# Message stage of a two-layer graph network: roots by logarithm and exponential on ScalarE, and one more sum on VectorE

## The reference, cut to what matters

```python
def logmap(x, y):
    xy = jnp.clip(mink_dot(x, y) + K, None, -EPS) - K
    u = y + xy * x * C
    normu = jnp.clip(mink_norm(u), MIN_NORM, None)   # a square root
    dist = jnp.sqrt(sqdist(x, y))                    # arcosh: a square root and a logarithm
    return proj_tan(dist * u / normu, x)
...
x_local_tangent = logmap(x[row], x[col])
cat = jnp.concatenate([x_tangent[row], x_tangent[col], distances], axis=-1)
h = jax.nn.silu(cat @ att_w1 + att_b1)
att = jax.nn.sigmoid(h @ att_w2 + att_b2) * edge_mask
agg = jax.ops.segment_sum(x_local_tangent * att, row, num_segments=N) / NORM_FACTOR
```

## Time and profile before

| | |
|---|---|
| Time, median of 3 runs | 3702.85 us (3699.55 to 3709.81) |
| Span of the profiled execution | 4137.2 us; no other time of that execution is given |
| VectorE busy over the span | 3401.4 us (82%) |
| TensorE busy over the span | 3002.7 us (73%) |
| ScalarE busy over the span | 2194.8 us (53%) |
| GpSimd busy over the span | 1969.1 us (48%) |

### The profile page before, as it was taken

How to read it: one execution, slowest core, us unless ns; L and a number is a source line. 1 busy time by engine, 2 the same in 40 slices (tenths; PEclk the granted TensorE clock), 3 DMA queues, 4 the chain that set the end, 5 groups by cost and what they waited for, 6 DMA issues and landing times. The chain is left out here.

```text
span 4137.2 us, 55464 instructions
## 1 busy us (share of the span) xinstructions
PE 3002.7 (73%) x12662; PEld 2413.6 (58%) x12662; DVE 3401.4 (82%) x9121; ACT 2194.8 (53%) x5961; POOL 1969.1 (48%) x2404
## 2 busy tenths in 40 slices
PE   3545444577777777677756688988988888888866
PEld 2434333455555555555545567777777777777754
DVE  8999996687888888788878378888888888888877
ACT  3235542444444444444438466666665666666557
POOL 1000003556666666666620366666666666666400
PEclk9867777788998889888988899999999999999988
DMA  2111004666667666666636655655655666556361
GB/s 65 39 55 38 13 26 148 191 202 208 202 208 216 207 209 208 211 205 209 206 98 174 172 161 168 173 163 168 171 168 167 167 172 170 166 167 170 89 145 50
DMA packets 295230, 635.60 MB, mean 154 GB/s; under 512 B 78197, under 2 KB 147123, under 8 KB 294657
## 3 DMA queue, kind: packets, MB, share of 16 engines
q0 software_dynamic: 141312, 463.96, 38.3%
q1 hardware_dynamic: 153602, 168.11, 14.5%
HBM read 587.26 MB, written 44.65 MB: 153 GB/s over the span
## 5 line engine op out<-in xcount | busy, mean ns | idle before, releaser
L2469 POOL DMA_INDIRECT area<-d_xr,col x880 | 890.2, 1012 | 686.8 <-DVE area L2706 236.8
L2562 PE MATMUL ms_near_a<-low,ms_hotT 128*128 x1760 | 550.4, 395 | 204.3 <-issue 99.2
L2066 PE MATMUL at_out<-at_pv,at_hot 128*128 128x264 f32 x1760 | 558.6, 447 | 75.7 <-issue 32.0
L2020 POOL DMA_INDIRECT low<-d_qv,col x440 | 449.6, 1022 | 265.6 <-DVE at_pv L2196 129.1
L2563 PE MATMUL ms_near_c<-tab_c,ms_hotT 128*128 x1760 | 536.1, 387 | 0.0
L2046 PE MATMUL at_kx<-area,tab_c 128*128 x1760 | 508.8, 417 | 21.8 <-issue 20.7
L2562 PEld LDWEIGHTS ms_near_a<-low,ms_hotT 128*128 128x128 f32 x1760 | 327.6, 192 | 301.6 <-issue 258.9
L2066 PEld LDWEIGHTS at_out<-at_pv,at_hot 128*128 128x128 f32 x1760 | 358.9, 217 | 161.9 <-issue 63.1
L2046 PEld LDWEIGHTS at_kx<-area,tab_c 128*128 128x128 f32 x1760 | 372.9, 213 | 96.0 <-issue 25.3
L2238 DVE SCALAR_TENSOR_TENSOR area<-area,tab_c,at_out 128x264 f32 x440 | 211.7, 481 | 216.4 <-remote 114.9
L2604 ACT COPY area<-area 128x2 f32<-128x2 f32 x440 | 82.0, 186 | 566.0 <-DVE area L2675 379.0
(11 more groups left out here) (375 smaller groups left out, 6560.6 us busy)
## 6 DMA issues: line engine op xcount, KB each, us to landing
tab_c<-by_dst_marks SPq DMA_DIRECT2D x110, 512.0 KB
ms_near_no<-by_src_near SPq DMA_DIRECT2D x110, 224.0 KB
area<-d_xr,col POOLq DMA_INDIRECT x880
d_qv<-low SPq DMA_DIRECT2D x10, 1120.0 KB, 5.0
low<-d_qv,col POOLq DMA_INDIRECT x448
d_xr<-mid_hm SPq DMA_DIRECT2D x5, 1128.8 KB, 6.8
first_x<-in_x_dram SPq DMA_DIRECT2D x5, 1120.0 KB
tab_c<-in_x_dram SPq DMA_DIRECT2D x5, 1120.0 KB, 7.0
```

The lines of the kernel that those rows point to most:

```text
L2020: pool.indirect_dma_start(out=ring[t.n % SLOTS][:, k, :], out_offset=None, in_=m.d_qv, in_offset=bass.IndirectOffsetOnAxis(ap=col[:, t.h, ...
L2066: last = TE.matmul(out[:, p % 2, 0:AW], hot[:, t.h % 2, j, :], pv[:, t.h % 2, j].rearrange("p h d -> p (h d)"), start=(k == 0), stop=(k == ...
L2469: pool.indirect_dma_start(out=far_rows(t, p)[:, k, :], out_offset=None, in_=m.d_xr, in_offset=bass.IndirectOffsetOnAxis(ap=col[:, t.h, SPA ...
L2562: TE.matmul(near_a[:, (SPAN * p + k) % 4, 0:TW], rows, m.tab_a[:, bass.ds(at, TW)], start=True, stop=True)
```

## The change

Two edits, both in `messages`.

First, the roots. ScalarE no longer has Sqrt. It loads the set that holds both Ln and Exp by name, takes Ln of two radicands at once (the scratch columns `R` and `NN` now lie side by side) and of the third, and one Exp with scale 0.5 over all three. The exponential of the attention follows in the same set. The logarithm moves behind `squares` of pair 1 into a function of its own, `log`, and the SiLU set is loaded right behind it. One semaphore, `root_in`, now tells of all roots, for VectorE and GpSimd alike.

Second, the far half. `dve_adds` says who adds it: VectorE for even pairs as before, and for pair 3 of a window's second group too, the group in whose turn no chain runs. TensorE leaves out its identity products there, ScalarE's SiLU takes the sum from SBUF, and `dve_added` counts VectorE's sums.

```diff
-        DD, Q, E, A, R, ROOT, U, NN, EX, Z, LN, S, OWN = (work[:, v, :] for v in range(13))
+        DD, Q, E, A, U, R, NN, ROOT, EX, Z, LN, S, OWN = (work[:, v, :] for v in range(13))
+        R_NN, ROOTS = work[:, 5:7, :], work[:, 5:8, :]
...
+        def dve_adds(t, p):
+
+            return p % 2 == 0 or p == SG - 1 and t.h % WG == 1
+
+        def dve_added(t, p):
+
+            return t.window * (SG + 1) + (t.h % WG) * (SG // 2) + p // 2 + p % 2 + 1
...
-                    reach(root_in, 2 * n + 2)
-                    reach(nn_in, n + 1)
+                    reach(root_in, n + 1)
...
-                        if p % 2:
+                        if dve_adds(before, q):
+                            pe.wait_ge(v_in, dve_added(before, q))
+                        else:
                             pe.wait_ge(silu_in, before.n * SG + q + 1)
-                        else:
-                            pe.wait_ge(v_in, before.n * (SG // 2) + q // 2 + 1)
-                    if p % 2:
+                    if not dve_adds(t, p):
                         got_rows(pe, t, p)
...
-                        if p % 2:
+                        if not dve_adds(t, p):
                             last = TE.matmul(near_c[:, p % 2, k * DIM:(k + 1) * DIM], m.ident[:, :], far_rows(t, p)[:, k, XB:XW],
                                              start=False, stop=True)
...
-                def chain(w):
+                def roots(w):
+
+
+
                     n = w.window
-                    act.wait_ge(ab_in, n + 1)
-                    AC.activation(R, R, ACT.Sqrt).then_inc(root_in, 1)
-                    AC.activation(ROOT, A, ACT.Sqrt, scale=2.0).then_inc(root_in, 1)
+                    AC.preload_act_table_set("natural_log_exp_and_others")
                     act.wait_ge(nn_in, n + 1)
-                    AC.activation(NN, NN, ACT.Sqrt).then_inc(norm_in, 1)
+                    AC.activation(R_NN, R_NN, ACT.Ln).then_inc(logs_in, 1)
+                    AC.activation(ROOT, A, ACT.Ln, scale=2.0).then_inc(logs_in, 1)
                     for t in (w, w.plus(1)):
                         AC.copy(dd[t.slot][:, :, DIM], A[:, (t.h % WG) * G:(t.h % WG) * G + G]).then_inc(a_in, 1)
+                    act.wait_ge(logs_in, 2 * n + 2)
+                    AC.activation(ROOTS, ROOTS, ACT.Exp, scale=0.5).then_inc(root_in, 1)
                     act.wait_ge(al_in, (w.n + WG) * G)
                     AC.activation(EX, AL[:, w.wslot, :], ACT.Exp, scale=-1.0, bias=nb2[:, 0:1]).then_inc(ex_in, 1)
-                    act.wait_ge(z_in, n + 1)
+
+                def log(w):
+                    act.wait_ge(z_in, w.window + 1)
                     AC.activation(LN, Z, ACT.Ln, bias=one).then_inc(ln_in, 1)
+                    AC.preload_act_table_set("silu_and_others")
...
                     if w:
-                        chain(w)
+                        roots(w)
                     squares(t, 1)
+                    if w:
+                        log(w)
...
-                    if p % 2 == 0:
+                    if dve_adds(t, p):
                         rows = far_rows(t, p)[:, :, XB:XW]
                         V.tensor_tensor(rows, rows, near_c[:, p % 2, :].rearrange("p (k d) -> p k d", d=DIM), ALU.add).then_inc(v_in, 1)
```

More of the change, by code:

```diff
@@ L2379, in messages @@
         got = [ctx.gather_sem(m, f"got{h}") for h in range(PAIRS)]
-        (c_in, made, hotT_in, near_in, apart, copied, squared, v_in, silu_in, al_in, dv, ab_in, root_in, nn_in, norm_in, ex_in, z_in, ln_in,
+        (c_in, made, hotT_in, near_in, apart, copied, squared, v_in, silu_in, al_in, dv, root_in, nn_in, logs_in, ex_in, z_in, ln_in,
          rden_in, a_in, pl, c_ready, weighted, out_in, summed) = (sem(n) for n in (
-             "c_in", "made", "hotT_in", "near_in", "apart", "copied", "squared", "v_in", "silu_in", "al_in", "dve", "ab_in", "root_in", "nn_in",
-             "norm_in", "ex_in", "z_in", "ln_in", "rden_in", "a_in", "pool", "c_ready", "weighted", "out_in", "summed"))
+             "c_in", "made", "hotT_in", "near_in", "apart", "copied", "squared", "v_in", "silu_in", "al_in", "dve", "root_in", "nn_in",
+             "logs_in", "ex_in", "z_in", "ln_in", "rden_in", "a_in", "pool", "c_ready", "weighted", "out_in", "summed"))
         def window_of(t):
@@ L2562, in near @@
                         TE.matmul(near_a[:, (SPAN * p + k) % 4, 0:TW], rows, m.tab_a[:, bass.ds(at, TW)], start=True, stop=True)
-                        last = TE.matmul(near_c[:, p % 2, k * DIM:(k + 1) * DIM], rows, m.tab_c[:, bass.ds(at, DIM)], start=True, stop=p % 2 == 0)
-                        if p % 2:
+                        last = TE.matmul(near_c[:, p % 2, k * DIM:(k + 1) * DIM], rows, m.tab_c[:, bass.ds(at, DIM)], start=True, stop=dve_adds(t, p))
+                        if not dve_adds(t, p):
                             last = TE.matmul(near_c[:, p % 2, k * DIM:(k + 1) * DIM], m.ident[:, :], far_rows(t, p)[:, k, XB:XW],
@@ L2614, in silu @@
                     else:
-                        act.wait_ge(v_in, t.n * (SG // 2) + p // 2 + 1)
+                        act.wait_ge(v_in, dve_added(t, p))
                         keep_node_term(t, p)
@@ L2663, in _ @@
                 V = nc.vector
-                PER = 13
+                PER = 14
                 def differences(t, p):
@@ L2744, in angles @@
                     ln.wait()
-                    V.scalar_tensor_tensor(R, T, 1.0, A, ALU.add, ALU.mult).then_inc(ab_in, 1)
+                    ln.mark(V.scalar_tensor_tensor(R, T, 1.0, A, ALU.add, ALU.mult))
                     ln.mark(V.scalar_tensor_tensor(U, A, 2.0, own, ALU.add, ALU.mult))
@@ L2757, in radii @@
                 def radii(w):
-                    dve.wait_ge(root_in, 2 * w.window + 2)
+                    dve.wait_ge(root_in, w.window + 1)
                     V.tensor_tensor(Z, A, R, ALU.add).then_inc(z_in, 1)
@@ L2764, in shares @@
                     n = w.window
-                    dve.wait_ge(norm_in, n + 1)
+                    dve.wait_ge(root_in, n + 1)
                     dve.wait_ge(ex_in, n + 1)
```

## The result

| kernel | median | lowest to highest | runs |
|---|---|---|---|
| before | 3703.72 us | 3699.55 to 3709.81 | 4 |
| after | 3675.89 us | 3674.21 to 3678.36 | 4 |

The ratio is 0.9923, with a 95% interval of 0.9909 to 0.9937. The kernel became faster by 28 us.

A forecast was written before the change was run, and what follows sets the result against it. The prediction took VectorE to bound the message stage in timed runs. It summed +33 us (added sum), -24 us (removed waits) and 0 for the rest to +9 us on 3703: 3712 us, range 3679 to 3738 us.

The forecast's parts named there:

- The pace: Message stage, timed runs: VectorE sets it, with 24.3 us of work and about 1 us of short waits a window.
- the wait of 4.38 us: VectorE's profiled wait before the differences of the next window's pair 0; claimed to be nearly gone in timed runs.
- ScalarE's chain: Roots to SiLU in each window: 2.57 us shorter, TensorE gets back 0.6 to 0.8 us, counted 0 in the sum.
- VectorE's removed waits: Second group, before pair 3's differences and before L2717: 0.22 and 0.21 us a window vanish, -24 us.
- VectorE's added sum: Pair 3 of each window's second group: one more tensor_tensor, a step of 0.60 us, +33 us in 55 windows.
- TensorE's removed products: Pair 3 of the second group: four passes fewer, 0.87 us less TensorE work a window, of which VectorE gets 0.43 us.
- What would show it: Signs in the changed profile: 275 second sums, 660 ident passes, two loads a window, VectorE busy 33 us more, short waits gone.
- The loads and roots: ScalarE: four table loads a window become two, 2.57 us less; last radicand to last root 0.9 us, covered by 2.6 us.
- Rival 1: Message stage: timed runs may lack the two short waits, so VectorE pays +33 us in full, 3736 us; chance 0.20.
- Rival 2: Second group: TensorE paces at a clock of about 0.96, and 0.87 us less a window gives 3655 us; chance 0.17.
- Rival 3: VectorE waits 0.3 us more a window for ScalarE's late SiLU; the change removes it, -17 us, 3695 us; chance 0.12.
- Rival 4: The new root chain holds GpSimd or VectorE by 0.5 us a window, +28 us, 3740 us; chance 0.06.

The follow-up runs named there:

- roots_only: The kernel after without its second half: VectorE adds for even pairs only, so the roots alone are changed; 3651.65 us.
- two_loads_third: The roots-alone kernel with two table loads put back behind the attention's exponential, so ScalarE has four again in a window; 3701.43 us.
- base_again: The kernel before, unchanged, run again for a profile of a timed run; 3705.47 us.
- log_in_chain_third: The roots-alone kernel with the logarithm back right behind the roots, ahead of the squares of pair 1; 3664.02 us.
- both_groups: The kernel after, with VectorE adding the far half of pair 3 in the first group of a window too; 3705.89 us.
- sum_only: The kernel before with only VectorE's added sum for pair 3 of the second group, roots and table loads as they were; 3701.50 us.
- sum_left_out_third: The roots-alone kernel with nobody adding the far half of pair 3 in the second group, that computation left out; 3657.55 us.

## Why the prediction was wrong

**The pace.** "In the timed runs the message stage goes at VectorE's pace, its 24.3 us of work and about 1 us of short waits in each window, 55 x 25.3." The size was right (25.28), and so was the guess that the wait of 4.38 us is no part of timed runs. What it named as the pace was not. The 1 us of short waits is no property of VectorE: it is how VectorE follows the other two engines. The window was the loop of ScalarE, TensorE and VectorE, in which TensorE lost 0.96 us before the product that needs SiLU of pair 3, on top of 24.3 us of passes. roots_only shows it (TensorE at 24.30 us without a gap), two_loads_third undoes it, and in the logarithm's experiment the same product is late again by as much as the window is longer.

**The step that failed** is in the part on ScalarE's chain: "it brings VectorE no more than those", that is, no more than the two waits of 0.43 us, which had already been counted for the removed products, and so 0 in the sum. Measured, it is the whole gain: -52 us. The mechanism was written down correctly: the 0.62 us of idle time before TensorE's product, the SiLU of pair 3 that it waits for, "so TensorE gets back 0.6 to 0.8 us as well". TensorE got 0.96 us back (0.70 of it listed as idle), and SiLU of pair 2 came 1.50 us earlier (+8.53 us from the window's start, then +7.03), where 1.5 had been worked out. Missing was the conclusion: at an engine with 24.25 us of work in a window of 25.3 a wait of 0.7 us is on the path, and VectorE, which waits for TensorE's sums right behind it, follows.

**VectorE's removed waits**, -24 us (0.22 + 0.21 us), were mis-sized. In the steps they are 1.15 us a window. The largest part left out was the 0.27 us before the sums of pair 2, which the prediction took as the loading of starts and left in. It is 0.38 us of a step and vanishes when nothing is late: on the mean of the windows, the step behind L2717 of pair 2 is 0.77 us where TensorE's last sum ended 0.45 us ahead of L2717 (base_again), and 0.39 us where it ended 1.0 to 1.35 us ahead (roots_only and log_in_chain_third). That the 0.55 us a window (1.15 - 0.60) make 30 us is no second test, as the 1.15 come from the same windows. And the waits go with the roots alone, not with the removed products.

**VectorE's added sum**, +33 us, had the right price. Its step is 0.60 us (2752.40 to 2753.00), and 0.65 us a window from after to both_groups. In after it costs 0.43 us over roots_only, by the medians 24 us. That TensorE's 24.30 us cover the rest there is an argument; the run that should have shown VectorE's pace without the sum did not do it cleanly. VectorE's busy time was to rise by 33 us, and rose by 8 in the 55 windows (0.14 us in each); part of the difference is that instructions overlap again where the waits were (L2734 lasts 0.47 us, and L2723 starts 0.40 us after it).

**TensorE's removed products**, 0.87 us: right as work, worth nothing. Once the roots are early, VectorE paces and TensorE waits 1.08 us a window. The counts of "What would show it" hold: the trace of after has 275 second sums (L2692) and 660 passes on ident (L2573), and two loads in a window.

**The loads and roots.** Two loads a window and 2.57 us less were right. The last root starts 0.43 us after the first Ln (2735.30 to 2735.73) and takes 0.24, so 0.7 us for an estimate of 0.9 (it ends at 2735.97, and the last radicand on VectorE at 2735.27), and VectorE did not wait; GpSimd did once, for 0.3 us. The rule of "ScalarE: Activation LUTs", "What ACT_TABLE_LOAD costs" in the Trainium skill, with a drain of some 1380 ns that goes with each load, was weighed there. The trace of after has 0.05 us between a load's end and the next function's start (2733.97 + 1.28 to 2735.30), and 0.02 us between the end of SiLU before it and its start (2733.36 + 0.59 to 2733.97), so it shows no drain either.

**The rivals.** Rival 1, VectorE pays in full: no, but both_groups shows its price from after on. (It stands at 3736 in the sum and at 3738 in the range; nothing hangs on the 2 us.) Rival 2, TensorE paces: the right sign, and TensorE is where the time was lost, but for the wrong reason. It was tied to a clock of 0.96, and the clock is 1.00 throughout; it took the gain from the removed products, and sum_only gives these 2 us of the 48. Rival 3, ScalarE's late SiLU: the right cause, looked for at VectorE, where it is 1.8 us in three waits, and not at TensorE, where it is 30.0 us in 43. Its 17 us were too small by a factor of three. Rival 4, late roots: VectorE never waits for a root between 2240 and 3320 us, and GpSimd waits for L2652 once in after (0.3 us) and 16 times in roots_only (4.9 us in 44 windows, 0.1 us in each), where the time is TensorE's passes all the same.

## What to carry to other kernels

When two engines have nearly the same work in a period, look for the one that waits for a third engine: here that wait was on the path, and the other one's short waits were only its shadow. Follow such a wait back around the period, from engine to engine, until it closes. An engine that is 73% busy can work without a pause in its part of the loop, and time on it was worth more here than work on the two that look full. Moving work from TensorE to VectorE cost 24 us in the second group and 30 us in the first once nothing else held them up. Compare the starts of matmuls too: a wait of a quarter of a microsecond did not show in the busy column. Before a sum is made on a profile whose span is far above the timed runs, get one that is near them, or take the idle times in it as open.

## What was not expected of the hardware

A tensor_scalar on VectorE that starts in a certain part of a GpSimd gather takes longer. In sum_left_out_third L2762 (128x16, 0.17 us by itself) took 0.39 us when it started 0.56 us into a gather, 0.30 us at 0.65 us, and in base_again and roots_only it took 0.21 us at 0.73 us: each time it ended 0.95 us after the gather's start. Started within the first 0.1 us of a gather, or 1.15 us after one's start, it took 0.17; and so did the other tensor_scalar instructions of this size that started 0.15 to 0.3 us or 0.81 to 0.87 us into one. The tensor_tensor instructions of 128x16 between them took 0.16 to 0.18 us in base_again and sum_left_out_third, wherever they started. The tensor_scalar of 128x128 is held as well: in base_again L2696 took 0.50 us for 0.34 when it started 0.49 us into a gather. The page "SBUF — State Buffer" of the Trainium skill (section "Who interferes with whom") has GpSimd and VectorE share a pair of ports as an exclusive lock for a whole instruction, which a tensor_scalar in a two-port mode needs, while a tensor_tensor with both inputs in SBUF needs only its read side. The common end agrees with such a lock; that starts in the first 0.3 us are not held does not, if the gather is one instruction that holds it throughout. No run here changed the mode to test it.

The kernel before takes 3705 us on two chips and 4200 on two others, 13% more. For the two-loads kernel, which has a trace on both kinds, the busy times of VectorE, ScalarE and GpSimd in 45 windows of the message stage agree within 0.5%.
